# Attention scores of two heads side by side in the row halves of TensorE

## What is computed

```python
q = (x @ wq.T).reshape(B, S, 16, 16)      # B = 2, S = 2048, head size 16
k = (x @ wk.T).reshape(B, S, 16, 16)
v = (x @ wv.T).reshape(B, S, 16, 16)
scores = jnp.einsum('bqhd,bkhd->bhqk', q, k) / sqrt(16)
probs = jax.nn.softmax(scores, axis=-1)
out = jnp.einsum('bhqk,bkhd->bqhd', probs, v).reshape(B, S, 256)
return out @ wo.T
```

## Time and profile before

| | |
|---|---|
| median of 3 runs | 3506.48 us (3504.53 to 3514.06) |
| profiled execution, its own time | 3506.37 us |
| its span | 3505.7 us |
| TensorE busy (share of span) | 2956.6 us (84%) |
| VectorE | 2483.4 us (71%) |
| ScalarE | 1861.5 us (53%) |
| first score to last score | 1323.5 to 2801.6 us |
| scores, exponentials | 2048 and 2048 |
| matmuls of the maxima, VectorE maxima | 2048 and 1024 |

### The profile page before, as it was taken

The page is one execution under the profiler, slowest core; times in us unless marked ns, Lnnn a source line. Parts: engine busy times, 40 slices in busy tenths (PEclk is TensorE's granted clock), DMA queues, the critical chain, the costliest instruction groups (busy, mean ns, idle before and its releaser), DMA issues. The chain is left out here.

```text
span 3505.7 us, 45186 instructions
## 1 busy us (share of the span) xinstructions
PE 2956.6 (84%) x12864; PEld 1137.4 (32%) x12865; DVE 2483.4 (71%) x2786; ACT 1861.5 (53%) x3378; POOL 1017.1 (29%) x548
## 2 busy tenths in 40 slices
PE   5789899889676749999999999999999863899990
PEld 1234343443233402222222222222222153566650
DVE  0699999999995688888888888888888065111113
ACT  3655665666541306777676767676777810222220
POOL 2888877877851210000000000000000035100006
PEclk8999999999988959999999999999999975999995
DMA  1111111111113420111111111100010036111114
GB/s 41 43 48 55 40 49 55 52 42 43 48 33 99 156 60 13 31 31 31 32 31 32 31 32 31 28 22 24 22 31 19 1 115 234 48 46 46 45 36 144
DMA packets 114924, 177.08 MB, mean 51 GB/s; under 512 B 26128, under 2 KB 73872, under 8 KB 114704
## 3 DMA queue, kind: packets, MB, share of 16 engines
q1 hardware_dynamic: 100880, 134.54, 13.0%
q0 software_dynamic: 13824, 39.86, 3.5%
HBM read 129.63 MB, written 44.43 MB: 50 GB/s over the span
## 5 line engine op out<-in xcount | busy, mean ns | idle before, releaser
L1417 DVE TENSOR_REDUCE nmh<-ring 128x2 f32<-128x1024 f32 x1024 | 1205.4, 1221 | 218.9 <-PE ring L1319 218.7
L1303 ACT ACTIVATE prob<-s_ps 128x512 f32<-128x512 f32 x2048 | 1061.4, 602 | 509.4 <-PE s_ps L1344 509.4
L767 DVE TENSOR_TENSOR_SCAN h<-dA,state,bx 128x512 f32<-128x512 f32 x512 | 618.0, 1264 | 116.2 <-ACT dA L606 115.6
L1344 PE MATMUL s_ps<-qs,ks 98*128 98x512 bf16 x2048 | 632.2, 388 | 23.5 <-issue 12.7
L391 POOL TENSOR_TENSOR bx<-u,bb 128x2048 f32<-128x2048 f32 x128 | 578.9, 4527 | 194.1 <-DVE h L767 193.9
L1356 PE MATMUL acc<-prob,vst 128*32 128x512 f32 x4096 | 551.2, 610 | 0.1
L1319 PE MATMUL ring<-k,q 64*128 64x512 bf16 x2048 | 417.0, 404 | 99.3 <-DVE nmh L1417 36.3
L606 ACT ACTIVATE dA<-dt,aneg 128x512 f32<-128x512 f32 x512 | 348.8, 691 | 270.4 <-DVE h L767 270.3
L673 PE MATMUL y_ps<-h,ident 128*128 128x512 f32 x1024 | 482.7, 616 | 1.1 <-DVE h L774 1.1
L1291 POOL COPY vst<-v_all 128x544 f32 (+1 forms) x16 | 10.2, 642 | 1386.2 <-PE acc L1356 1386.2
L1344 PEld LDWEIGHTS s_ps<-qs,ks 98*128 98x128 bf16 x2048 | 154.0, 97 | 647.5 <-ACT prob L1303 450.3
(11 more groups left out here) (218 smaller groups left out, 2395.9 us busy)
## 6 DMA issues: line engine op xcount, KB each, us to landing
bb<-b_rows SPq DMA_DIRECT2D x128, 256.0 KB, 3.2
parts<-part POOLq DMA_DIRECT2D x48, 256.0 KB, 2.8
qs<-parts SPq DMA_DIRECT2D x192, 64.0 KB, 2.2
ks<-parts SPq DMA_DIRECT2D x192, 64.0 KB, 2.2
xt<-slots_in POOLq DMA_DIRECT2D x72, 128.0 KB, 2.3
slots_out<-yt SPq DMA_DIRECT2D x72, 128.0 KB, 1.7
q<-parts SPq DMA_DIRECT2D x128, 64.0 KB, 2.2
k<-parts SPq DMA_DIRECT2D x128, 64.0 KB, 2.2
```

The costliest lines, as they stand in the source:

```text
L767: nc.vector.tensor_tensor_scan(h[:, n % HR, d, :], dA[:, d % 2, :], bx[:, n % BR, d, :], state[:, b, n, d:d + 1], ALU.mult, ALU.add).then_ ...
L1303: nc.scalar.activation(prob[:, k % PR, j, :], s_ps[:, m % SR, :], ACT.Exp, scale=SC).then_inc(s_exp, 1)
L1344: nc.tensor.matmul(s_ps[:, m % SR, :], ks[:, par, hh, t * P:(t + 1) * P], qs[:, par, hh, j * CH:(j + 1) * CH], start=True, stop=True).then ...
L1417: nc.vector.tensor_reduce(nmh[:, :, t, at], ring[:, s, :, :], AX.X, ALU.max, negate=True).then_inc(s_free[s], 1)
```

## The change

The two heads of a pair are now worked on together. The steps of a pair run over query halves: steps 0 to 15 are queries 0 to 1023, steps 16 to 31 the others. The four scores of a step are two heads times two blocks of 512 queries, in the order head 0, head 1, head 0, head 1. The 98 rows are split in two: `qa`/`ka` hold the first four parts (64 rows), `qb`/`kb` the last two and the maximum (34 rows), with head 0 from partition 0 and head 1 from partition 64. So a block takes four matmuls in place of two: two with 64 rows, one for each head and each in its row half, then two with 34 rows that add to the same banks. In this text A0 A1 B0 B1 are those of the first block, A2 A3 B2 B3 those of the second. `outputs` scales the result in two VectorE instructions, since its queries lie differently in `att`. The number of loads, exponentials, maxima and V matmuls stays the same.

```diff
-        qs = sb("qs", [ROWS, 2, 2, L], BF16)
-        ks = sb("ks", [ROWS, 2, 2, L], BF16)
+        qa = sb("qa", [P, 2, L], BF16)
+        ka = sb("ka", [P, 2, L], BF16)
+        qb = sb("qb", [P, 2, L], BF16)
+        kb = sb("kb", [P, 2, L], BF16)
...
                 for hh in range(2):
-                    load(qs, 0, (par, hh), 0, Q_PARTS, n, s_op[par])
-                    load(ks, 0, (par, hh), 1, K_PARTS, n, s_op[par])
+                    load(qa, par, hh, 0, Q_PARTS[0:4], n, s_op[par])
+                    load(ka, par, hh, 1, K_PARTS[0:4], n, s_op[par])
+                    load(qb, par, hh, 0, Q_PARTS[4:6], n, s_op[par])
+                    load(kb, par, hh, 1, K_PARTS[4:6], n, s_op[par])
...
-            def scores(n, par, k, j):
-                m = QC * k + j
-                hh, t = k // KT, k % KT
-                back = m - SR if m >= SR else max(x for x in range(NU) if x % SR == m % SR) - NU
-                wait(pe, s_exp, NU * n + back + 1)
-                nc.tensor.matmul(s_ps[:, m % SR, :], ks[:, par, hh, t * P:(t + 1) * P],
-                                 qs[:, par, hh, j * CH:(j + 1) * CH], start=True, stop=True).then_inc(s_S, 1)
+            def scores(n, par, k, jj):
+                half, t = k // KT, k % KT
+                at = slice(t * P, (t + 1) * P)
+                to = slice((2 * half + jj) * CH, (2 * half + jj + 1) * CH)
+                for hh in range(2):
+                    m = QC * k + 2 * jj + hh
+                    back = m - SR if m >= SR else max(x for x in range(NU) if x % SR == m % SR) - NU
+                    wait(pe, s_exp, NU * n + back + 1)
+                    r = slice(64 * hh, 64 * hh + 4 * HD)
+                    nc.tensor.matmul(s_ps[:, m % SR, :], ka[r, par, at], qa[r, par, to], start=True, stop=False)
+                for hh in range(2):
+                    m = QC * k + 2 * jj + hh
+                    r = slice(64 * hh, 64 * hh + 2 * HD + 2)
+                    nc.tensor.matmul(s_ps[:, m % SR, :], kb[r, par, at], qb[r, par, to], start=False, stop=True
+                                     ).then_inc(s_S, 1)
...
-                    v0 = hh * (HD + 1)
+                    v0 = (j % 2) * (HD + 1)
...
                 for k in range(KK):
                     scores(n, par, k, 0)
+                    use_ring(k, 0)
                     scores(n, par, k, 1)
-                    use_ring(k, 0)
-                    scores(n, par, k, 2)
-                    scores(n, par, k, 3)
                     use_ring(k, 1)
...
-                nc.vector.tensor_tensor(dst, got[:, :, :, 0:HD], r[:, :, :, None].to_broadcast([P, TT, QC, HD]),
-                                        ALU.mult).then_inc(s_free[s], 1)
+                for jj in range(2):
+                    t0 = (2 * half + jj) * TT
+                    dst = att[:, bass.ds(n, 1), t0:t0 + TT, :].rearrange("p a c (h w) -> p (a c) h w", h=2)
+                    last = nc.vector.tensor_tensor(
+                        dst, got[:, :, 2 * jj:2 * jj + 2, 0:HD],
+                        r[:, :, 2 * jj:2 * jj + 2, None].to_broadcast([P, TT, 2, HD]), ALU.mult)
+                last.then_inc(s_free[s], 1)
```

More of the change, by code:

```diff
@@ L1113, in attention_stage @@
     assert NMAX == KK and QC == 4 and NP % 2 == 0 and NP >= 6
-    ROWS = 6 * HD + 2
     SC = float(HD) ** -0.5
@@ L1220, in _, with load @@
         def _(sp):
-            def load(dst, at, par_hh, m, order, n, s):
+            def load(dst, par, hh, m, order, n, s):
                 for g, part in enumerate(order):
[L1224 to L1227, removed]
+                    src = parts_dram[m, part, bass.ds(n * 2 * HD + hh * HD, HD), :]
+                    sp.dma_start(dst[64 * hh + g * HD:64 * hh + (g + 1) * HD, par, :], src).then_inc(s, 16)
             def load_stack(n, par):
@@ L1239, in load_lead @@
                 for hh in range(2):
-                    load(q4, 64 * hh, (par, hh), 0, Q_PARTS[0:4], n, s_op4[par])
-                    load(k4, 64 * hh, (par, hh), 1, K_PARTS[0:4], n, s_op4[par])
+                    load(q4, par, hh, 0, Q_PARTS[0:4], n, s_op4[par])
+                    load(k4, par, hh, 1, K_PARTS[0:4], n, s_op4[par])
             def max_rows(n, par, fills):
@@ L1246, in max_rows @@
                     for s in range(2):
-                        sp.dma_start(qs[6 * HD + s:6 * HD + s + 1, par, hh, :],
+                        sp.dma_start(qb[64 * hh + 2 * HD + s:64 * hh + 2 * HD + s + 1, par, :],
                                      nmr[hh * KT:(hh + 1) * KT, s, :]).then_inc(s_mr[par], 16)
@@ L1279, in _ @@
             nc.gpsimd.memset(vst[:, :, :, :], 0.0).then_inc(s_one, 1)
-            for par in range(2):
-                pool.wait_ge(s_one, par + 1)
-                nc.gpsimd.memset(ks[6 * HD:6 * HD + 2, par, :, :], 1.0).then_inc(s_one, 1)
+            for hh in range(2):
+                pool.wait_ge(s_one, hh + 1)
+                nc.gpsimd.memset(kb[64 * hh + 2 * HD:64 * hh + 2 * HD + 2, :, :], 1.0).then_inc(s_one, 1)
             pool.wait_ge(s_id, 1)
@@ L1326, in rows_of_max, with outputs @@
                 nc.tensor.transpose(ring[0:2 * KT, 0, 0, 0:P], nm[:, :], ident[:, :]).then_inc(s_full[0], 1)
-            def outputs(ct, n, hh):
-                s = 1 - hh
+            def outputs(ct, n, half):
+                s = 1 - half
                 wait(pe, s_free[s], ct.next(s) - 1)
-                wait(pe, s_o, 2 * n + hh + 1)
+                wait(pe, s_o, 2 * n + half + 1)
                 for t in range(TT):
-                    last = nc.tensor.transpose(ring[:, s, 0, t * P:(t + 1) * P], osb[:, hh, t * P:(t + 1) * P],
+                    last = nc.tensor.transpose(ring[:, s, 0, t * P:(t + 1) * P], osb[:, half, t * P:(t + 1) * P],
@@ L1347, in values @@
             def values(n, par, k):
-                hh, t = k // KT, k % KT
+                half, t = k // KT, k % KT
                 if t == 0:
-                    wait(pe, s_o, 2 * n + hh)
+                    wait(pe, s_o, 2 * n + half)
                 if k == 0:
@@ L1440, in outputs, with read_acc @@
                 got = ring[:, s, 0, :].rearrange("p (c j w) -> p c j w", c=TT, j=QC)
-                r = rec[:, hh, :].rearrange("p (c j) -> p c j", j=QC)
+                r = rec[:, half, :].rearrange("p (c j) -> p c j", j=QC)
                 nc.vector.reciprocal(r, got[:, :, :, HD]).then_inc(s_rec, 1)
-                wait(dve, s_rec, 2 * n + hh + 1)
-                dst = att[:, bass.ds(n, 1), :, hh * HD:(hh + 1) * HD].rearrange(
-                    "p a (j c) w -> p c (a j) w", c=TT)
-                nc.vector.tensor_tensor(dst, got[:, :, :, 0:HD], r[:, :, :, None].to_broadcast([P, TT, QC, HD]),
-                                        ALU.mult).then_inc(s_free[s], 1)
-            def read_acc(n, hh):
-                wait(dve, s_pv, KK * n + KT * (hh + 1))
-                nc.vector.tensor_copy(osb[:, hh, :], acc[:, :]).then_inc(s_o, 1)
+                wait(dve, s_rec, 2 * n + half + 1)
+                for jj in range(2):
[5 more added lines that the diff above has]
+                last.then_inc(s_free[s], 1)
+            def read_acc(n, half):
+                wait(dve, s_pv, KK * n + KT * (half + 1))
+                nc.vector.tensor_copy(osb[:, half, :], acc[:, :]).then_inc(s_o, 1)
             def prologue():
```

## The result

The changed kernel takes 3665.74 us (3664.6 to 3669.59), the kernel before 3506.48 us: ratio 1.0452, 95% interval 1.0433 to 1.0471. It is 159 us slower. Forecast were 3674 us, or +168.

The account below looks back on a forecast made before the run. TensorE's fixed order bounds the kernel, with the second block waiting for the first score's exponential. 142.7 + 4.5 + 12 + 1 = 160 us, a quarter of the way towards 195: +168, so 3674 us; own range 3655 to 3710, 8 in 10 3630 to 3760.

Parts of the forecast that it names:

- The wait of A3: Ordinary step: A3 must wait for the first score's exponential to free its bank, until 1.30 us after A0.
- last pair: Final pair of heads, 31 steps without maxima: from 2.46 to 2.84 or 2.90 us each, +12 to +14 us.
- The work behind it: Ordinary step, from A3 to the next A0: B2 and B3 0.22, M1 0.22, V 0.32 and 1.00, together 1.76 us.
- The savings: Ordinary step: three of five changes of kind between TensorE's matmuls go, about 0.30 us on paper.
- The rule on weight loads: Skill's rule: a weight load overlaps matmuls in flight only in another row group; three loads of 0.10 would join the chain.
- rival 1: Weight loads of B0, B3 and M1 aren't hidden in halves: step 3.36 us, kernel about 3800 us; chance 10%.
- rival 2: Row halves don't run together for accumulating scores: step 3.50 us, kernel 3855 us; chance 4%.
- Rivals 3 and 4: Rival 3 (5%): A3's wait doesn't bind, 3375 us. Rival 4 (8%): work passes the waiting A3, 3571 us.
- rival 5: TensorE's granted clock falls to half, V takes 1.00 us more each step: over 3900 us; chance 2%.
- the long rhythm: Ordinary steps with the later exponential start (0.49 in place of 0.43): 3.12 us in place of 3.06, sum +195 us.
- irregular extra: Extra time in ordinary steps beyond the pair's typical length (ends of the loop, clock): forecast +1 us.
- special steps: Steps 2, 18 and 28 of 15 pairs: about 0, 0.5 later and -0.20 us each; together +4.5 us (+3 to +9).

Follow-up runs that it names:

- head-by-head run: Changed kernel with the matmuls of each block in the order A0 B0 A1 B1 in place of A0 A1 B0 B1: 3669.27 us, ratio 1.0460.
- the kernel with its maxima together: Kernel before with both maxima of a step between its second and third score, in every step: 3465.34 us, ratio 0.9878.
- the version that keeps the old order in step 18: Kernel before with both maxima between the second and third score, except in step 18: 3455.30 us, ratio 0.9860.
- the short exponential: Changed kernel with half of each exponential left out (columns 0 to 255 of 512 computed): 3564.27 us, ratio 1.0167.

## Why the prediction was right, step by step

**The wait of A3.** Forecast at 1.30 after A0 by 0.22 + 0.43 + 0.60 + 0.05. It came at 1.29, released by ScalarE. That this wait sets the step is shown from four sides: a shorter exponential shortens the step by its own 0.21; work put ahead of A3 is free (M1, 0.21 a step); undoing the two-matmul scores brings 2.72 back; and splitting V so that the bank is free in time takes 0.39 off. The last pair, which has no maxima, shows the same: its step went from 2.46 to 2.89, and TensorE stands for 0.53 ahead of A3, where it stood for 0.32. This is one of its steps in the changed kernel:

```profile
2941.25 0.39 PE L1349 MATMUL s_ps<-qa,ka 64*128 64x512 bf16 x2
...
2942.61 0.39 PE L1349 MATMUL s_ps<-qa,ka 64*128 64x512 bf16 x1 [0.53 <-ACT prob L1304]
```

**The work behind it.** Forecast 1.76, measured 1.75. That B2 needn't count, since head 1's half is the chain, was argued from the order; the head-by-head run shows it.

**The savings.** Three changes of kind per step are gone, as the 0.22 between scores and maxima shows. Two of the three lay ahead of A3, where TensorE then waited for longer; the third shows only in the 0.22 from B3 to M1. In the kernel with its maxima together one change of kind fewer, off the wait, brought 0.10 a step at once.

**The rule on weight loads.** The loads of B0 and B1 start at 2332.33, when the matmuls of A0 and A1 run in the same row halves, and B follows A by 0.22. So rival 1 is out: the loads are hidden. The rule of the Trainium skill ("TensorE: Matmul & The Clock Gate", Part 3) isn't borne out by this trace.

**The other rivals.** Halves run together (rival 2 is out: 0.39 covers A0 and A1). Rivals 3 and 4 needed A3 ahead of the first exponential's end, or matmuls that pass A3 while it waits for ScalarE; neither is seen. The clock (rival 5) stayed at 0.99.

**The sizes.** The forecast was 168 us because it went a quarter of the way to the long rhythm, and that share stayed as it was before: without this 9 us the sum was 160, against 159. That these two are so close is in part luck: against the forecast column of the table the ordinary steps are 1.8 us lower, the irregular extra 4.0 lower, the special steps 1.7 higher, the last pair 1.5 higher, and 1.8 us lie outside the stage, for which I had nothing. Among the special steps, step 28 was mis-sized. It got 0.47 shorter, not 0.20 (4.30 to 3.83, medians over the pairs): the row of maxima is computed 0.45 after the step's start, where it was at 0.66 to 0.72, because VectorE, with more idle time, is no longer behind. The first line is of the kernel before, in a step that starts at 2058.91, the others are of the changed kernel:

```profile
2059.63 0.28 DVE L1423 TENSOR_REDUCE nm<-nmh 128x32 f32<-128x128 f32 x1
...
2132.48 0.39 PE L1349 MATMUL s_ps<-qa,ka 64*128 64x512 bf16 x2
...
2132.92 0.28 DVE L1430 TENSOR_REDUCE nm<-nmh 128x32 f32<-128x128 f32 x1
```

Against it stands step 18: +0.48 was forecast well at 0.5 in the typical pair, but in five of 15 pairs the clock fell behind it (below). The two errors, -4 and +4 us, nearly cancel. The 1.7 us that are left are step 2, for which I had nothing.

## What to carry to other kernels

When a result is split over two accumulating matmuls, the throughput of TensorE may be the same, but the consumer starts one matmul later, and so does everything that waits for the freed bank. With three banks for four products a step, look for the product that reuses the step's own first bank, add up its chain (matmul, delay, consumer, delay), and put work that doesn't depend on it, here the maxima or half of V, ahead of it in the queue. And before taking changes of kind out of a queue, see whether they lie under a wait: here two changes of kind saved under a wait were worth nothing, while a single one saved where TensorE ran through was worth 0.10 us a step, 1.4% of the kernel in the version that keeps the old order in step 18.

## What was not expected of the hardware

In the changed kernel the granted clock falls to half behind the output of step 18 in five of 15 pairs, though the stage as a whole has 0.99. One such place (two stretches: length, busy time and count of TensorE first, and the clock after POOL's), with the V that it lengthened, 1.66 in place of 1.06:

```profile
2099.00:2103.00 4.00, 2.75 (x24) 1.06 (x24) 2.40 (x6) 2.17 (x4) 0.00 (x0) 1.00 0.03 6
2103.30:2106.50 3.20, 3.20 (x17) 0.62 (x11) 1.44 (x2) 0.97 (x2) 0.00 (x0) 0.50 0.00 0
```

```profile
2102.55 0.39 PE L1320 MATMUL ring<-k,q 64*128 64x512 bf16 x2 [0.99 <-DVE att L1454]
...
2102.87 1.66 PE L1365 MATMUL acc<-prob,vst 128*32 128x512 f32 x8
```

TensorE was busy 2.75 of 4.00 us ahead of the fall: A3's wait of 0.26 and one of 0.99 for VectorE lie close together. The kernel before has the second (1.08) but not the first, and in the same step its clock stayed at full speed in every pair. The price is 1.2 to 1.4 us each time: 0.6 to 1.0 in the step itself (5.4 to 5.8 us, against 4.73 to 4.79 in the other pairs) and 0.4 to 0.6 in the next one.

The two pauses together might be taken for the cause, but the other runs don't bear this out. Head by head, TensorE as a whole stands still for only 0.04 ahead of A3, since B2 fills the time, and for 0.99 behind the transposes; the clock fell there in four of 15 pairs. With the short exponential in the changed kernel the two pauses are 0.04 and 0.99 as well, and it fell in none. With the maxima ahead of the second block the pause is 1.54, and with the maxima together in the kernel before it is 1.33; it fell in one pair each. The cause stays open.
